# A four-layer conditioned transformer, 16 attentions and 16 feed-forward parts: where the normalized rows of the item two ahead are transposed

## What is computed

```
mod = silu(cond) @ w_ada + b_ada                      # six vectors of 288 per sequence
h   = layernorm(x) * (1 + scale1) + shift1
q, k, v = h @ w_qkv + b_qkv                           # 16 heads of 18
x   = x + gate1 * (softmax(q k^T / sqrt(18)) v @ w_proj + b_proj)
h   = layernorm(x) * (1 + scale2) + shift2
x   = x + gate2 * (gelu(h @ w1 + b1) @ w2 + b2)       # hidden 1152
```

## Time and profile before

| | us |
|---|---|
| median of 3 runs | 2263.82 |
| lowest, highest run | 2252.39, 2264.69 |
| span of the profiled execution | 2257.0 |
| its own time | not listed apart from the three runs |
| PE busy | 2033.0 (90%) |
| DVE busy | 1335.6 (59%) |
| ACT busy | 1143.6 (51%) |

### The profile page before, as it was taken

One profiled execution on the slowest core, in us unless ns is written; L12 is line 12 of the kernel. 1 busy time (PEld: TensorE's weight loads), 2 busy tenths in 40 slices (PEclk: granted clock), 3 DMA queues, 4 the chain that ended last, 5 costly groups with the idle time before them and its releaser, 6 DMA issues.

```text
span 2257.0 us, 38969 instructions
## 1 busy us (share of the span) xinstructions
PE 2033.0 (90%) x15592; PEld 1509.0 (67%) x15592; DVE 1335.6 (59%) x2940; ACT 1143.6 (51%) x1705; POOL 207.4 (9%) x311
## 2 busy tenths in 40 slices
PE   6978899899989998999799899899888898999898
PEld 4347388658966994788375657788786556464658
DVE  4757637756774767476556673462444849484833
ACT  2444624574655456445626464552443464637373
POOL 2000001202100211012010000011000000000001
PEclk9787989899989999999889999998898998999999
DMA  5333332343333233333322313346254141314011
GB/s 158 77 123 57 100 95 72 79 111 86 89 77 106 72 89 76 96 94 88 94 72 35 103 17 65 73 88 109 34 95 130 7 121 26 99 11 115 9 14 25
DMA packets 204731, 173.97 MB, mean 77 GB/s; under 512 B 54822, under 2 KB 164678, under 8 KB 204550
## 3 DMA queue, kind: packets, MB, share of 16 engines
q1 hardware_dynamic: 197974, 158.76, 30.1%
q0 software_dynamic: 6576, 12.71, 2.1%
HBM read 125.57 MB, written 40.11 MB: 73 GB/s over the span
## 4 chain that ended last, share of the span: by engine, by line
PE 63%; DVE 18%; ACT 12%; DMA 3%; issue 2%; SPq 2%; POOL 0%; ACTq 0%; POOLq 0%; DVEq 0%
PE PSA L1856 16%; PE PSA L1871 13%; DVE MX L1496 7%; PE PSA L1647 5%; PE PSA L1760 5%; PE PSA L1737 5%; ACT PB L1345 4%; PE PSA L1707 4%; PE PSA L1750 4%; PE PSA L1719 2%; DVE FL L1396 2%; PE PSA L1780 1%; ACT FH L1375 1%; PE PSA L1670 1%; DVE HH L1626 1%
## 5 line engine op out<-in xcount | busy, mean ns | idle before, releaser
L1496 DVE TENSOR_REDUCE MX<-PSA 128x1 f32<-128x512 f32 x768 | 490.4, 682 | 296.9 <-PE PSA L1737 293.2
L1856 PE MATMUL PSA<-A,FH 128*128 128x256 f32 x2520 | 445.3, 292 | 12.5 <-DVE HH L1626 9.6
L1871 PE MATMUL PSA<-FH,HH 128*128 128x288 f32 x2016 | 447.7, 313 | 2.0 <-DVE HH L1626 2.0
L1382 ACT ACTIVATE HH<-PSA 128x512 fp32r<-128x512 f32 x252 | 150.4, 597 | 572.5 <-PE PSA L1856 567.3
L1345 ACT ACTIVATE PB<-PSA 128x1024 f32<-128x1024 f32 x384 | 370.9, 1025 | 102.5 <-PE PSA L1750 101.8
L1856 PEld LDWEIGHTS PSA<-A,FH 128*128 128x128 f32 x2520 | 364.9, 195 | 34.6 <-issue 17.3
L1871 PEld LDWEIGHTS PSA<-FH,HH 128*128 128x128 f32 x2016 | 329.7, 195 | 42.3 <-issue 38.0
L1871 PE MATMUL PSA<-FL,HH 128*128 128x288 f32 x1008 | 303.7, 301 | 0.0
L1737 PE MATMUL PSA<-KS,QS 54*128 54x512 f32 x768 | 226.1, 517 | 40.0 <-DVE MX L1496 14.0
L1255 POOL TENSOR_TENSOR X<-X,TM 128x288 f32<-128x288 f32 x128 | 101.1, 808 | 1496.7 <-DVE TM L1561 1496.6
L1760 PE MATMUL PSA<-PB,VT 128*32 128x512 f32 x1536 | 219.6, 637 | 0.0
(11 more groups left out here) (166 smaller groups left out, 2261.5 us busy)
## 6 DMA issues: line engine op xcount, KB each, us to landing
qkd<-HH SPq DMA_DIRECT2D x48, 504.0 KB
ST<-in_L_cond_w SPq DMA_DIRECT2D x51, 432.0 KB
ST<-in_L_cond_w SPq DMA_DIRECT2D x102, 192.0 KB
QS<-qkd SPq DMA_DIRECT2D x88, 144.0 KB
KS<-qkd SPq DMA_DIRECT2D x88, 144.0 KB
QS<-qkd SPq DMA_DIRECT2D x144, 72.0 KB
KS<-qkd SPq DMA_DIRECT2D x144, 72.0 KB
ST<-in_L_cond_w SPq DMA_DIRECT2D x153, 48.0 KB
```

Of the source, the lines that this page charges most:

```text
L1382: e.activation(r(HH[u][:, 0, :]), PS[bk][:, :], gelu)
L1496: e.reduce_max(MX[p // 2 % 2][:, col:col + 1], PS[bk][:, :], axis=AX.X).then_inc(free[bk], 1)
L1856: m = e.matmul(PS[bk][:, s_ * 256:(s_ + 1) * 256], r(w_), r(x_[:, half * 256:(half + 1) * 256]), start=(z == 0), stop=(z == 6))
L1871: m = e.matmul(PS[bk][:, 0:C], r(HH[u][:, c, tk]), r(w_), start=False, stop=(j == NCH - 1 and z == 2))
```

## The change

The condition at the end of `mid(i)` now holds for every item that has one two ahead. The wait for the last `fc1` of the feed-forward part of the phase stays.

```diff
@@ -748,7 +748,7 @@
         if i + 1 < NI:
             gates(i + 1, 0)
             yield
-        if (i + 1) // 4 == 2:
+        if i + 2 < NI:
             while last_fc1[0] < i - 1:
                 yield
             yield from turn_x(norm_of[i + 2], i % 2, (i + 2) // 4, 0, (i + 2) % 4)
```

## The result

The changed kernel takes 2290.2 us (median of 4 runs, 2281.6 to 2298.3), the kernel before, run beside it, 2261.1 us. The ratio is 1.0129, 95% interval 1.0094 to 1.0165: slower by 1.3%, or 29 us. The profiled run of the changed kernel was its slowest, 2298.3 us; the span is 39.6 us longer than in the earlier trace rows, so the profiles show some 10 us more than the medians do. They also differ by 8 us before the first change in the order of work: from the start to the first value projection of item 1 it is 139.8 us before and 147.7 after.

What follows compares the result with a forecast made beforehand. PE, busy 90% of the span, bounds the kernel; only its 224 us idle can change. Terms -30 - 3.3 + 11.1 + 0 + 3.8 + 10.5 + 4.9 + 4.6 + 3.4 = +5.0 us took 2263.82 to 2269; range 2244 to 2290.

Steps and rivals of the forecast that it cites:

- The step that failed: First-pass steps moved to the previous attention's tail: same work, maxima covered by the length of a step, cost nothing.
- rival C: Cold starts: half clock in attentions' first steps, 8 us, and for projections now in them, 12 us; 2289, chance 0.27.
- -30 us in the attentions: Ten attentions each lose 1.8 us of transposes and a 1.2 us wait before the first projection: -30 us.
- -3.3 us, row DMAs early: Early issue brings the last row DMAs forward, removing PE's waits for them in 4 cases: -3.3 us.
- Phases 1 to 3, +3.7 each: Phase ends: third copy waits for backlogged DVE, casts and exps queue behind it; +3.7 us each, +11.1 together.
- Phase 4, nothing: Phase end: ACT's 6.59 us wait for weights from DRAM covers the added work; 0, upper bound 3.8 us.
- Phases 5, 6 and 13, 3.9 each to the exps (3.5 in the sum): Phase ends: DVE's maxima and chunks delay first exps by 3.9 us, less 0.4 of old idle; +10.5 together.
- Phase 11, +4.6: Phase end: `XN` completes late and transposes now precede the attention's first scores; exps 4.6 us later.
- Phase 12, +4.9 in all: Phase end: 3.5 us of delay plus 1.4 for casts of two more weight pieces behind the third copy.
- Phase 0, +3.8: Chunks precede the split freeing the weight buffer on a DVE without gaps, so weights come later: +3.8 us.
- +3.4, waits for line 1490 in layer 0: Three projections instead of two share banks with first-pass scores: one more 0.9 us wait in four attentions, +3.4 us.
- Rival B at 2242: Phase ends: DVE is not behind, so added work is mostly hidden, 11.0 us exposed; -22 us, 2242, chance 0.22.

Runs made afterwards that it cites:

- g1_hold4: The changed kernel with only the projections of the next item held to the fifth step instead of the third: 2257.6 us, ratio 1.0008.
- f1_before_land8: The kernel before, with only the first-pass scores of head groups 0 and 1 put 4 us of planned TensorE time earlier: 2287.0 us, ratio 1.0130.
- e1_hold: The changed kernel with the projections of the next item held to their old seventh step, early turns kept: 2272.7 us, ratio 1.0070.
- e5_landg: The changed kernel with first-pass scores of head groups 0 and 1 put 8 us of planned TensorE time later, except item 12: 2318.4 us, ratio 1.0278.
- e11_hold8: The changed kernel with the projections held to the ninth step, two later than before the change: 2326.5 us, ratio 1.0294.
- e3_hf3: The changed kernel with a third scratch, the idle tile OS, for the third chunk's copy: 2288.6 us, ratio 1.0143.
- e7_warm: The changed kernel with the last first-pass matmul repeated ten times before attentions 6, 7, 13 and 14: 2287.6 us, ratio 1.0136.
- f2_defer_hold4: The changed kernel with DVE's casts and subtractions put behind the attention's first steps, third copy in OS, projections from the fifth step: 2241.2 us, ratio 0.9928.

## Why the prediction was wrong

**The step that failed** is the one costed at nothing: "First-pass steps that move from the head of one attention to the tail of the one before are the same work, and I cost that at nothing: what covers their maxima is the length of a step". I asked only what covers DVE. Those steps also need the projected columns back from DRAM, and PE reached them before these had landed: 12.3 us of waits in eight of the ten attentions, where the kernel before had none. Taking the turns out of the attention pulled the projections four steps forward (seventh to third) and the first pass with them (thirteenth or fourteenth to ninth or tenth). With the projections two steps later and all else as changed (g1_hold4), the loss of 1.29% falls to 0.08%, and by the profiles the attentions take 34.4 us less than before, where I forecast 30 less. The forecast of +5 us lies within the interval of g1_hold4, whose projections start at the fifth step; the code of the change put them at the third. That agreement is in part luck: of g1_hold4's profile, attentions, ends and phase 0 add to +7.2 against the kernel before, and the stretches that the forecast did not price, the start included, to -11.5.

How the columns come back is plain in SP's timeline in attention 6 of the changed kernel, with PE's first score of item 7 behind it:

```profile
1253.38 0.32 SPq L1077 DMA_DIRECT2D qkd<-HH  x1
1261.05 2.10 SPq L1104 DMA_DIRECT2D QS<-qkd  x6
1263.18 2.15 SPq L1104 DMA_DIRECT2D KS<-qkd  x6
...
1268.91 0.80 PE L1737 MATMUL PSA<-KS,QS 54*128 54x512 f32 x2 [1.10 <-DMA KS<-qkd]
```

The loads begin 7.7 us after the store that they wait for, their issue takes 4.3 us, and the score runs 15.5 us after the store. The Trainium skill ("DMA: Bandwidth & Descriptors", section "🔬 Anatomy of one DMA — SWDGE (gpsimd) path") says that the time beyond the bytes of a DMA is mostly the receipt of its last write, heaviest for DRAM, and that the issuing sequencer, not the DMA engine, waits on semaphores. These stores are issued by SP, not by GpSimd, so it bears on them by analogy. The waiting on the sequencer agrees: the profile has line 1104 on SP wait for the landing of these stores, up to 7.2 us. The share of the receipt doesn't: the core's DMA engines are busy for 0.60 or more of each microsecond up to 1259.4, so most of the 7.7 us here has packets moving, the store's or those of DMAs before it.

What share of the loss from the third to the fifth step is which: the ten attentions differ by 37.3 us in the two profiles. Waits for columns are 12.3 us of it (12.3 to nothing; with the one at the start it is 15.8 to 1.9) and waits at line 1707 for line 1490 are 9.0 us (13.6 to 4.6). Why the latter are fewer no run shows: both orders have three projections in a row. Over the ten attentions together, the granted clock is the half one (1.2 GHz) for 74 us before, 122 us after the change and 93 us in g1_hold4. By the two levels, 29 us less at the half clock are worth at most 14 us, an estimate that would about make up the rest. These are differences of two profiles, and waits and clock moved together; that waits for columns are path is shown by f1_before_land8.

The other way to read g1_hold4 and e1_hold is rival C's: that they took the projections out of the half clock of the first steps. The trace settles that. The seven matmuls of line 1707 in the third step take 1.9 us in eight attentions of the changed kernel and 2.2 in attention 2 (attention 7 has none); before, in the seventh step, they took 1.9 in all nine. The busy time of that line's two groups in the whole run is 133.8 us before, 134.8 after and 134.3 in g1_hold4. C had 12 us for it.

**Point by point.**
- *-30 us in the attentions.* Near in size, wrong in condition: -34.4 in g1_hold4, -26.7 with the old step, +2.9 in the change. The transposes did leave.
- *-3.3 us, row DMAs early.* Waits of line 1750 for them went from 3.3 to 1.9 us. Of no weight; but e5_landg and e11_hold8 show 22.7 and 40.9 us of them when the projections leave their place.
- *Phases 1 to 3, +3.7 each.* Exps counted from the last fc2 came 0.4 us earlier, 3.3 and 4.1 later. The chain through the third copy is there, and without it (e3_hf3) the exps of attentions 3 and 4 come only 2.0 and 1.2 later; the rest of the delay is another's. Wrong for phase 1, right in size for 2 and 3. e3_hf3 shows no gain in the whole time from it.
- *Phase 4, nothing.* The exps came 1.5 us earlier, but PE's first score 3.2 later. *Phases 5, 6 and 13, 3.9 each to the exps (3.5 in the sum):* +4.0, +3.9, +4.2. *Phase 11, +4.6:* +5.7. *Phase 12, +4.9 in all:* +4.2. Near.
- *Phase 0, +3.8.* Mis-sized: +8.2 to the first score. I thought of the weights; the DVE work also stands in front of the remainders that fc2 reads, which is 2.6 us of it. PE at the end of phase 0:

```profile
241.26 0.81 PE L1871 MATMUL PSA<-FH,HH 128*128 128x288 f32 x2 [2.62 <-DVE HH L1626]
```

- *+3.4, waits for line 1490 in layer 0.* +4.1 (9.5 to 13.6), 17 cases instead of 11. Near in size.
- *Rival B at 2242.* Its sign did not come: ACT's idle time before line 1284 put down to line 1463 is 12.5 us, 2.2 before. Its sum also leaves out, without a reason, the +3.4 that the forecast has; with it B would be at 2245.
- *Rival C at 2289.* The time agrees with 2290 and two of its signs came: the granted clock over the first three steps of attentions 6 and 14 is 0.69 and 0.65, where the earlier trace rows has 0.79 and 1.00. But its main term, 12 us for projections at the half clock, came as 1 us, as shown above. What grew at the lower clock are the scores and values of lines 1750 and 1760, by 22.7 us together. I gave C 0.27 for a price that came out right mostly for other reasons; that is luck.
- *The rule on psum-queue cycling* (the Trainium skill, "TensorE: Matmul & The Clock Gate", section "A second HAM failure mode: psum-queue depth-cycling") would have put the time near C. The trace has more half clock in the changed kernel; e7_warm removed two thirds of a pause and the clock did not come back, and in f2_defer_hold4 the same pause went with either clock. No run here shows that the pauses are the cause.
- *First in, first out on ACT and DVE.* The third copy with the casts and exps behind it at 670.08 agrees.

What stays open: why the clock falls at one handover and not at another, how much of the loss in the changed kernel is the clock's by itself, since every run that took away waits also changed the clock, and what made the rest of the phases 11.6 us shorter.

## What to carry to other kernels

When steps are taken out of a stream that a planner fills, everything behind them moves forward, and each follower has to be priced by what it waits for, DMA round trips included. Sweep the start of the followers before judging the move: here steps 3, 5, 7 and 9 gave 1.0129, 1.0008, 1.0070 and 1.0294 for the same work. Work moved to a seam between stages should be split by engine: leaving DVE's casts behind the seam, with the third copy freed of its wait, won about 1% with the projections at the seventh step (1.0070 to 0.9975). Together with the fifth step and without the turn in phase 11, a loss of 1.3% became a gain of 1%.

## What the runs showed of the hardware

A store to DRAM and the load that reads it back took 15.5 us from the store's issue to the first matmul that uses the data, with 4.3 us of that for issuing twelve loads on one queue. DMAs behind such loads on SP's queue were issued after them: row DMAs whose data were ready at 701.7 us went out at 706.5. Putting the user of such data 4 planned us earlier cost 27.5 us, with 23.7 us more of waits. Ten repeated matmuls in a pause of PE left the granted clock behind it at 0.67. With the same matmuls and the same 1.49 us of idle time in front, it was 1.00 behind one handover and 0.62 behind another.
